# Two layers of attention on one Trainium2 core: the low half of the probabilities moves from VectorE to GpSimd

## What is computed

```python
x = x + xattn0(layernorm(x), ctx, mask)   # 16 heads of 32, masked softmax over the 77 keys
x = x + ffn0(layernorm(x))                # rows quantised to 8 bits, ternary weight 512 x 512, + bias
x = x + xattn1(layernorm(x), ctx)         # 16 heads of 64, softmax over 77 keys, output weight, + bias
x = x + ffn1(layernorm(x))                # fft(x) @ w, real(ifft(.)), + bias
...
scores = einsum('bqhd,bkhd->bhqk', q, k)
weights = softmax(scores, axis=-1)
ctx = einsum('bhqk,bkhd->bqhd', weights, v)
```

## Time and profile before

| | us |
|---|---|
| median of three runs | 1199.66 (1199.63 to 1200.8) |
| profiled execution, its own time | 1197.73 |
| its span in the trace | 1195.9 |
| mean granted clock | 0.91 |

### The profile page before, as it was taken

The page is one execution under the profiler, slowest core; times in us unless marked ns, Lnnn a source line. Parts: engine busy times, 40 slices in busy tenths (PEclk is TensorE's granted clock), DMA queues, the critical chain, the costliest instruction groups (busy, mean ns, idle before and its releaser), DMA issues. The chain is left out here.

```text
span 1195.9 us, 17258 instructions
## 1 busy us (share of the span) xinstructions
PE 971.4 (81%) x6035; PEld 512.5 (43%) x6035; DVE 925.0 (77%) x1728; ACT 637.6 (53%) x1660; POOL 396.7 (33%) x341
## 2 busy tenths in 40 slices
PE   1896987874877969996999699969987997789794
PEld 1442464332443544453445344534444454334441
DVE  8777388567989699969988897899699968935722
ACT  2333174344676377639654964687368537514601
POOL 0214023112533345343524441454154424602402
PEclk9988997995977988998999799979998999899797
DMA  9623036345555656656575658465746564550612
GB/s 365 184 83 106 1 72 158 96 126 130 89 103 109 112 92 118 131 108 113 105 133 112 107 101 163 86 120 101 146 85 120 102 107 83 97 100 19 117 42 70
DMA packets 379024, 131.92 MB, mean 110 GB/s; under 512 B 365149, under 2 KB 370813, under 8 KB 375610
## 3 DMA queue, kind: packets, MB, share of 16 engines
q1 hardware_dynamic: 378937, 130.82, 52.4%
HBM read 35.14 MB, written 15.96 MB: 43 GB/s over the span
## 5 line engine op out<-in xcount | busy, mean ns | idle before, releaser
L630 POOL TENSOR_TENSOR pr<-pr,sm 128x616 f32<-128x616 f32 x128 | 167.5, 1309 | 463.3 <-DVE sm L1131 456.3
L730 ACT ACTIVATE pr<-scores,mx,factor 128x77 f32<-128x77 f32 x512 | 204.4, 421 | 58.4 <-DVE mx L1119 58.4
L167 PE MATMUL wb<-xT,wq_hl 128*128 128x512 f16 x384 | 150.2, 391 | 4.1 <-DMA xT<-xh 4.1
L168 PE MATMUL wb<-xT,wq_hl 128*128 128x512 f16 x384 | 149.1, 388 | 0.0
L169 PE MATMUL wb<-xT,wq_hl 128*128 128x512 f16 x384 | 148.7, 387 | 0.0
L743 ACT ACTIVATE ph<-pr 128x618 f16<-128x618 f32 x128 | 92.7, 724 | 88.0 <-DMA prT<-ph 77.3
L167 PE MATMUL scores<-k1b,qc 128*128 128x154 f16 x256 | 62.9, 262 | 89.5 <-ACT pr L730 88.6
L1136 DVE SCALAR_TENSOR_TENSOR ph<-pr,ph 128x618 f16<-128x618 f32 x128 | 127.9, 999 | 3.1 <-ACT ph L743 3.0
L1070 DVE SCALAR_TENSOR_TENSOR xr<-wb,factor,xr 128x512 f32<-128x512 f32 x72 | 52.9, 739 | 84.9 <-PE wb L169 84.9
L621 POOL TENSOR_TENSOR rstd<-var,mhalf 128x2 f32<-128x2 f32 (+1 forms) x48 | 53.3, 1110 | 183.6 <-DVE var L1028 183.6
L730 ACT ACTIVATION_READ_ACCUMULATOR pr<-scores,mx,factor 128x1 f32 x512 | 107.9, 211 | 0.0
(11 more groups left out here) (220 smaller groups left out, 2524.8 us busy)
## 6 DMA issues: line engine op xcount, KB each, us to landing
xr<-in_x SPq DMA_DIRECT2D x6, 1024.0 KB, 5.6
out_x<-xr SPq DMA_DIRECT2D x6, 1024.0 KB, 5.5
prT<-in_dft SPq DMA_DIRECT2D x1, 3072.0 KB, 22.5
k1b<-scr_k SPq DMA_DIRECT2D x16, 154.0 KB, 6.8
scr_v<-k1b SPq DMA_DIRECT2D x9, 256.0 KB, 2.8
scr_k<-k1b SPq DMA_DIRECT2D x7, 308.0 KB, 3.1
xr<-in_wf SPq DMA_DIRECT2D x2, 1024.0 KB, 10.6
x<-in_x SPq DMA_DIRECT2D x2, 1024.0 KB, 10.6
```

The costliest lines, as they stand in the source:

```text
L167: pe.matmul(out, lhs(0), rhs(0), start=start, stop=False, **kw)
L168: pe.matmul(out, lhs(0), rhs(1), start=False, stop=False, **kw)
L630: pool.tensor_tensor(v, v, s, ALU.mult).then_inc(probs_ready, 1)
L730: ins = act.activation(pr[U % 3][:, h // 4, cols], sc[:, U % 2, h // 4, cols], ACT.Exp, bias=mx[:, U % 4, h:h + 1], scale=k["factor"][:, f ...
```

## The change

The set `LOW_BY_POOL` names all sixteen units. For them GpSimd makes the low half, in a new function `probs_low` behind the slot's `rstd_of` and ahead of its bias additions. Its instruction takes two operands and one operation, so the factor `PS` moves: VectorE multiplies the sums by 1/`PS` before the reciprocal (one more instruction of 8 columns), so that `pr` holds `PS` times the probability after `normalise`, and ScalarE's copy has scale 1.0. VectorE's L1136 is no longer executed. The semaphore `probs_lo` becomes two, for which a function of the same name gives semaphore and count. `rstd_of` also waits for `ln_lowered` where VectorE makes the rows.

```diff
@@ -118,6 +118,7 @@
 LN0_STATS = 8
 HEADWISE = {("X", 0), ("X", 2), ("X", 5), ("X", 7), ("Y", 0), ("Y", 2), ("Y", 3), ("Y", 5)}
 ROWS_BY_DVE = {(2, 2)}
+LOW_BY_POOL = {("X", u) for u in range(8)} | {("Y", u) for u in range(8)}
 APPLY = {2: [(2, 2)], 8: [(1, 0)], 10: [(3, 0)], 11: [(0, 0)], 12: [(0, 2)], 13: [(1, 2)], 14: [(3, 2)], 16: [(2, 0)]}
 LOWER = {2: [(2, 2)], 9: [(1, 0)], 10: [(3, 0)], 11: [(0, 0)], 12: [(0, 2)], 13: [(1, 2)], 15: [(3, 2)], 17: [(2, 0)]}
 BIAS = {7: [(2, 2)], 10: [(1, 0)], 12: [(3, 0)], 14: [(1, 2)], 17: [(2, 0), (3, 2)]}
@@ -287,7 +288,7 @@
         bank_full, bank_hi, bank_free = sem("bank_full"), sem("bank_hi"), sem("bank_free")
         scores_full, shifted, exp_done, sums_ready, probs_ready = (sem(n) for n in (
             "scores_full", "shifted", "exp_done", "sums_ready", "probs_ready"))
-        probs_hi, probs_lo = sem("probs_hi"), sem("probs_lo")
+        probs_hi, lo_by_dve, lo_by_pool = sem("probs_hi"), sem("lo_by_dve"), sem("lo_by_pool")
         turned = [sem(f"turned{u}") for u in range(8)]
         ln_var, rstd_ready, ln_ready, ln_applied, ln_lowered, biased = (sem(n) for n in (
             "ln_var", "rstd_ready", "ln_ready", "ln_applied", "ln_lowered", "biased"))
@@ -411,6 +412,11 @@
 
             return [v for v in UNIT if UNIT[v] == n][0]
 
+        def probs_lo(n):
+
+            by_pool = unit_numbered(n)[:2] in LOW_BY_POOL
+            return lo_by_pool if by_pool else lo_by_dve, sum(1 for v in UNIT if UNIT[v] <= n and (v[:2] in LOW_BY_POOL) == by_pool)
+
         def unit_at(g):
 
             return SLOT_UNIT[g] if 0 <= g < len(SLOTS) else None
@@ -488,7 +494,7 @@
             def turn(stage, u, b):
                 t, half = unit_place(stage, u)
                 U = UNIT[stage, u, b]
-                sp.wait_ge(probs_lo, U + 1)
+                sp.wait_ge(*probs_lo(U))
                 reader = ("Y", "pv", 4 * half + 3, b - 2) if stage == "X" else ("X", "pv", t, b + 1)
                 if reader in FILL:
                     sp.wait_ge(bank_full, FILL[reader] + 1)
@@ -618,6 +624,9 @@
                 pool.wait_ge(ln_var, n + 1)
                 if b > 0:
                     pool.wait_ge(ln_applied, APPLIED[j, t0 + width - 2, b - 1] + 1)
+                    for pair in range(t0, t0 + width, 2):
+                        if (j, pair) in ROWS_BY_DVE:
+                            pool.wait_ge(ln_lowered, APPLIED[j, pair, b - 1] + 1)
                 pool.tensor_tensor(rstd[:, j, ts], var[:, j, ts], mhalf[:, ts], ALU.pow).then_inc(rstd_ready, 1)
                 pool.wait_ge(rstd_ready, n + 1)
                 pool.tensor_tensor(shift[:, j, ts], mean[:, j, ts], rstd[:, j, ts], ALU.mult).then_inc(ln_ready, 1)
@@ -628,6 +637,12 @@
                 v = pr[U % 3][:, :, 0:GK].rearrange("p g (h n) -> p g h n", h=4)
                 s = sm[:, U % 4, :].rearrange("p (g h u) -> p g h u", g=2, u=1).broadcast_to([P, 2, 4, KEYS])
                 pool.tensor_tensor(v, v, s, ALU.mult).then_inc(probs_ready, 1)
+
+            def probs_low(stage, u, b):
+                U = UNIT[stage, u, b]
+                pool.wait_ge(probs_hi, U + 1)
+                pool.tensor_tensor(ph[:, U % 2, 1, :, :, 0:CH], pr[U % 3][:, :, 0:GKP].rearrange("p g (c n) -> p g c n", c=3),
+                                   ph[:, U % 2, 0, :, :, 0:CH], ALU.subtract).then_inc(lo_by_pool, 1)
 
             def add_bias(j, pair, b):
                 pool.wait_ge(ln_lowered if (j, pair) in ROWS_BY_DVE else ln_applied, APPLIED[j, pair, b] + 1)
@@ -658,6 +673,8 @@
                 for e in groups_at(g):
                     if e[0] != 0 or e[3] != 0:
                         rstd_of(*e)
+                if unit_at(g - 2) and unit_at(g - 2)[:2] in LOW_BY_POOL:
+                    probs_low(*unit_at(g - 2))
                 for e in listed(BIAS, g):
                     add_bias(*e)
 
@@ -724,7 +741,7 @@
                 f = F_E0 if stage == "X" else F_E1
                 if (stage, u) in HEADWISE:
                     if U >= 3:
-                        act.wait_ge(probs_lo, U - 2)
+                        act.wait_ge(*probs_lo(U - 3))
                     for h in range(8):
                         cols = slice((h % 4) * KEYS, (h % 4 + 1) * KEYS)
                         ins = act.activation(pr[U % 3][:, h // 4, cols], sc[:, U % 2, h // 4, cols], ACT.Exp, bias=mx[:, U % 4, h:h + 1],
@@ -741,7 +758,7 @@
                     before = [v for v in UNIT if UNIT[v] == U - 2][0]
                     act.wait_ge(turned[before[1]], 16 * (PASS[before] + 1))
                 act.activation(ph[:, U % 2, 0, :, :, 0:CH], pr[U % 3][:, :, 0:GKP].rearrange("p g (c n) -> p g c n", c=3), ACT.Copy,
-                               scale=PS).then_inc(probs_hi, 1)
+                               scale=1.0 if (stage, u) in LOW_BY_POOL else PS).then_inc(probs_hi, 1)
 
             def ln_apply(j, pair, b):
                 n = APPLIED[j, pair, b]
@@ -1120,7 +1137,7 @@
                     return
                 m = mx[:, U % 4, :].rearrange("p (g h u) -> p g h u", g=2, u=1).broadcast_to([P, 2, 4, KEYS])
                 if U >= 3:
-                    dve.wait_ge(probs_lo, U - 2)
+                    dve.wait_ge(*probs_lo(U - 3))
                 dve.tensor_tensor(four(pr[U % 3][:, :, 0:GK]), s, m, ALU.subtract).then_inc(shifted, 1)
 
             def sums(stage, u, b):
@@ -1128,13 +1145,15 @@
                 dve.wait_ge(exp_done, U + 1)
                 if (stage, u) not in HEADWISE:
                     step(dve.tensor_reduce(sm[:, U % 4, :].rearrange("p (g h) -> p g h", g=2), four(pr[U % 3][:, :, 0:GK]), AX.X, ALU.add))
+                if (stage, u) in LOW_BY_POOL:
+                    step(dve.tensor_scalar(sm[:, U % 4, :], sm[:, U % 4, :], 1.0 / PS, None, ALU.mult))
                 dve.reciprocal(sm[:, U % 4, :], sm[:, U % 4, :]).then_inc(sums_ready, 1)
 
             def probs_low(stage, u, b):
                 U = UNIT[stage, u, b]
                 dve.wait_ge(probs_hi, U + 1)
                 dve.scalar_tensor_tensor(out=ph[:, U % 2, 1, :, :, 0:CH], in0=pr[U % 3][:, :, 0:GKP].rearrange("p g (c n) -> p g c n", c=3),
-                                         scalar=PS, in1=ph[:, U % 2, 0, :, :, 0:CH], op0=ALU.mult, op1=ALU.subtract).then_inc(probs_lo, 1)
+                                         scalar=PS, in1=ph[:, U % 2, 0, :, :, 0:CH], op0=ALU.mult, op1=ALU.subtract).then_inc(lo_by_dve, 1)
 
             def ln0(b):
                 dve.wait_ge(x_loaded, 16 * (b + 1))
@@ -1173,7 +1192,7 @@
                     sums(*unit_at(g - 1))
                 for use in SLOT_DRAINS[g]:
                     low(use)
-                if unit_at(g - 2):
+                if unit_at(g - 2) and unit_at(g - 2)[:2] not in LOW_BY_POOL:
                     probs_low(*unit_at(g - 2))
                 if s == LN0_STATS and there(i + 1) and i + 1 > 0:
                     ln0(i + 1)
```

## The result

The changed kernel takes 1257.89 us (median of four runs, 1254.9 to 1258.87) against 1199.64: the ratio is 1.0488, with a 95% interval of 1.0469 to 1.0507. That is 58 us slower, where 22 were forecast. The profiled execution took 1257.88 us, its span is 1256.1.

The account below looks back on a forecast made before the run. TensorE (81% busy) was taken to bound, idling mostly for ScalarE's exponentials, with VectorE late at three places a round. Terms 15 + 4.8 - 2 - 1 + 5.5 = +22.3 us gave 1222 us, range 1205 to 1240.

Parts of the forecast that it names:

- The sum: Whole kernel: 15 + 4.8 - 2 - 1 + 5.5 = +22.3 us.
- block of iteration 1: Iteration 1: GpSimd's subtraction of X2 stands behind all-reduce and reload, so clearing `k1b` and all behind it slip, +15 us.
- the clock: Iteration 1's stall: granted clock is already 0.5 there, so nothing was added for the clock.
- the ring of `pr`: Iteration 1: X1's subtraction must be done before VectorE shifts X4's scores, limiting relief there to 0 to 1.4 us.
- GpSimd's gaps with the releaser "issue": Iteration 1, around GpSimd's all-reduce and reload: gaps of 5.96 and 7.00 us have no wait in them.
- A middle round: Six middle rounds: 0.7 us gain ahead of quantising, late transposes giving back more; -0.4 each (-1.5 to +2), -2 in six.
- sign of being wrong: Whole forecast: wrong if clearing does not move against the transposes, or if rounds change by over 2 us.
- The rival of mutual holding: Rounds: GpSimd and VectorE hold each other, 2.5 us more lost each, 15 in six: 1237 us; chance 0.17.
- Iteration 0: End of its X units: late GpSimd subtractions delay X7's transpose, for which TensorE waits; +4.8 us, 3.5 to 6.5.
- The rest of iteration 1: Iteration 1 outside the block: the same relief of VectorE, -1 us, 0 to -3.
- The end: After the last X units: TensorE waits directly for Y7's (+3.5) and Y3's (+2) transposes; +5.5 us, 3 to 8.
- The rival that relief wins: Rounds: quick subtractions let each gain 5.4 us, six 33, giving 1191 us; chance 0.07.

Follow-up runs that it names:

- e1: Changed kernel without the low half on either engine, its waiters waiting for ScalarE's high half, one bias row loaded for three: 1155.29 us, ratio 0.9637.
- e2: As the kernel without low halves, but GpSimd does a same-shaped subtraction on tiles of its own that nobody waits for: 1198.77 us, ratio 1.0003.
- e12: Changed kernel with only another memory layout for five small VectorE operations: 1245.52 us, ratio 1.038.
- e3: Changed kernel with four buffers of `pr` in place of three, one bias row loaded for three: 1249.09 us, ratio 1.0426.
- e5: Kernel with GpSimd's unread subtraction, five small VectorE operations in another layout, the subtraction's operands from a weight tile: 1180.31 us, ratio 0.9843.

## Why the prediction was wrong

**What the 60 us of span are made of.** The measured 1257.89 us lie 18 us above the upper end of the range, 1240. TensorE's waits for transposes of probabilities grew by 33.7 us, and not in two places: 7.9 up to X0 of iteration 1, 6.9 between X5 of iteration 1 and X7 of iteration 2, 9.2 in the five rounds, 8.9 at the end. The sum had 4.8 and 5.5 for them. Those for ScalarE's exponentials grew by 14.6 in the block of iteration 1, as forecast, and fell by 10.8 in the rounds, where the relief shows. Those for shifted scores grew by 10.7, 6.9 of them in the rounds; the sum had nothing for them. And TensorE's own work grew by 11.7, 6.2 in the rounds and 3.9 at the end. So what failed is, by size: the wait for GpSimd's low half, which the prediction called what counts and then priced in too few places; the clock and the ring of `pr`, both put at nothing; and GpSimd's load on VectorE, put at nothing.

**Iteration 1, the block: right.** Clearing was to start at about 302 after 20 us of waiting, and TensorE to stand some 27; it was 306.11, 21.07 and 27.23. The stretch lost 16.5 us against 15, and moving the all-reduce gave 13.6 back. The reading that nothing shortens GpSimd's gaps with the releaser "issue" held: 5.80 and 6.97 us.

**A middle round: the step that failed most.** -0.4 us was put, +2.9 measured, more than the 2 that the prediction named as its sign of being wrong. The term of relief was VectorE's 0.8 us a unit at three places, worth at most 2.5 and taken as 0.7; GpSimd's load was put at nothing but queueing; the late transposes were to give back 0.3 beyond a gain of 1.3. The runs show 5.1 us a round for relief without any wait (e1), a load of 6.3 (e2) and waits of 1.7: the first two are each far more than was put and nearly cancel, at +1.2 where -0.7 was put, and the waits add the rest. The load was left out of the sum, and kept as a rival, because `tensor_scalar` was not seen to be held. That was read from L1043 alone, and the prediction says itself that no L1043 stood beside GpSimd's work. The trace of before had it, in a line that the prediction does not read:

```profile
L1039 DVE TENSOR_SCALAR cscale<-amax,factor x16: 228/229/1183, 198.9 to 1014.5; 128x2 f32<-128x2 f32 x16
```

Its longest is five times its shortest, for 2 columns; 2 of the 16 are over 1.1 us. The prediction added 128 operations of this kind and put 180 us of GpSimd's work beside them all. So "VectorE is relieved of 102 us" became 30. What the holding of five such operations costs in the change is 12.4 us (e12), a fifth of the whole.

**The rival of mutual holding** had the mechanism and the direction. Its price was 2.5 us a round more than forecast; it was 3.3 for load and waits together, so the price is near by luck: of it e12 gives holding 1.2 a round. It also expected GpSimd's operations to lengthen to 1.8 us, which they did not (1.37 in the mean): it is VectorE that is held, for the most part.

**Iteration 0: mis-sized.** 4.8 us (3.5 to 6.5) against 8.2. The last wait was to be 8 us and was 8.53. But TensorE now also waits 3.65 us at 184.79 for transposes of X2 and X3 (the fill `pv` 1), 1.04 before, an earlier place of the same kind that was not looked at.

**The rest of iteration 1: wrong sign.** -1 was put where 8.3 were lost (with a part of a round). Load and relief cancel here (-0.3 in e2), the waits cost 8.6: TensorE waits 6.9 us more for transposes, and e3 puts 6 of the 9 us of the ring of `pr` (its three buffers in turn) here. That ring was named once, for X4, and priced nowhere else.

**The end: mis-sized.** 5.5 (3 to 8) against 12.7. TensorE's three waits for transposes, the first before, then all three after:

```profile
1027.13 0.38 PE L167 MATMUL wb<-prT,v1b 103*128 103x512 f16 x1 [1.99 <-DMA prT<-ph]
```

```profile
1081.22 0.58 PE L168 MATMUL wb<-prT,v1b 103*128 103x512 f16 x1 [5.46 <-DMA prT<-ph]
...
1104.80 0.59 PE L168 MATMUL wb<-prT,v1b 103*128 103x512 f16 x1 [4.77 <-DMA prT<-ph]
...
1179.36 0.58 PE L168 MATMUL wb<-prT,v1b 103*128 103x512 f16 x1 [3.18 <-DMA prT<-ph]
```

The wait for Y7 grew from 2.34 to 4.77, by 2.4 where 3.5 was put, and the one for Y3 of the last batch from 0.17 to 3.18, by 3.0 where 2 was put: 5.4 together, as forecast, by errors that cancel. The place one batch before it, from 1.99 to 5.46, was left out. With these 8.9 us and the 3.9 of TensorE's own work the stretch is accounted for, but for small terms that cancel.

**The clock: put at nothing, from one slice.** In the stretch of the block that was right: TensorE is busy 22.8 us in both. Elsewhere it was not. The matmul at 1027.13 in the trace of before takes 0.38 us, the one at 1081.22 after the change 0.58. In the 2 us from there the granted clock is 0.83 and 0.50, and in the 5 us ahead TensorE was busy for 1.49 us and not at all. Over the whole trace 236 matmuls take over 1.5 times the median of their group, against 200 before. Summed over all that exceed their median by 30% or more, the excess is 79.9 us against 69.2, which accounts for most of the 11.7. No run set the clock by itself, so what any one wait costs by way of it stays open.

**The rival that relief wins** was priced at 33 us less in six rounds; e1, which waits for no low half, gives 26 in five. The relief is real, and GpSimd's presence takes as much.

## What to carry to other kernels

Before moving work from VectorE to GpSimd, ask the trace for the shortest and longest of every VectorE line that will run beside it, the smallest ones first: an operation of 0.17 us that stands in a chain can be held for 1.1. Then try the move once with its result unread: that tells load from waits before either is mended. A gain of 43 us without the load was nothing with it. And where a result that is awaited in every unit moves to a busier queue, price the wait at each of its readers, not only where one stands out already: here it was the larger part.

## What the runs showed that was not expected

- A `tensor_scalar` on 2 columns beside GpSimd's subtraction has a median of 854 ns with equal counts on both sides, and one on 6 columns 159 ns with outermost counts of 3 and 6; a reciprocal on 8 columns stays at 202 to 205 ns.
- Where the small operations are no longer held, a larger one behind them is, more than before: the scaling of 512 columns behind them went from 16.1 to 24.5 us for 32 (e2, e5), and still the kernel was 18.5 us faster.
- GpSimd, with 147 us more work, has the 48 bias additions of the earlier trace rows in the mean shorter than before (1.37 against 1.50 us), while the 24 of the other bias are not (1.47 against 1.45). With VectorE's L1136 gone it may be held less itself; no run took that apart.
